# Mirrored blocks of the diagonal score quarters turned by VectorE and DMA in place of TensorE, 36 score blocks multiplied where 38 were, and the row maxima subtracted out of place into a ring of three tiles

## The reference, cut to what matters

```python
lhs = x * w_lhs
rhs = x * w_rhs
scores = jnp.einsum('nsd,ntd->nst', lhs, rhs)
attn = jax.nn.softmax(scores, axis=2)
return jnp.einsum('nst,ntd->nsd', attn, x)
...
h = jax.nn.relu(jnp.einsum('bsh,hi->bsi', hidden_states, W1) + b1)
return jnp.einsum('bsi,ih->bsh', h, W2) + b2
```

## Time and profile before

| what | value |
|---|---|
| median of three executions | 693.37 us |
| profiled execution, span from first to last instruction | 691.5 us |
| instructions | 13488 |
| TensorE matmuls busy | 686.1 us, 99% |
| VectorE busy | 558.4 us, 81% |
| ScalarE busy | 427.5 us, 62% |
| GpSimd busy | 361.7 us, 52% |
| DMA traffic | 77.54 MB, mean 112 GB/s |

### The profile page before, as it was taken

How to read it: one execution, slowest core, us unless ns; L and a number is a source line. 1 busy time by engine, 2 the same in 40 slices (tenths; PEclk the granted TensorE clock), 3 DMA queues, 4 the chain that set the end, 5 groups by cost and what they waited for, 6 DMA issues and landing times.

```text
span 691.5 us, 13488 instructions
## 1 busy us (share of the span) xinstructions
PE 686.1 (99%) x4621; PEld 627.7 (91%) x4621; DVE 558.4 (81%) x1059; ACT 427.5 (62%) x625; POOL 361.7 (52%) x396
## 2 busy tenths in 40 slices
PE   9999999999999999999999999999999999999998
PEld 8688899998999989998999989999899998999997
DVE  5699989799898898978989799887989887876421
ACT  3265398736786367683786647864678634845562
POOL 3572576636654386352872458643665434523644
PEclk9999999999999999999999999999999999999999
DMA  8211761137431382315622266112843126003300
GB/s 294 81 49 59 204 193 55 39 107 252 123 100 56 103 232 91 99 61 179 180 67 90 67 226 185 61 38 98 258 121 99 46 91 221 1 1 100 100 31 30
DMA packets 61663, 77.54 MB, mean 112 GB/s; under 512 B 5632, under 2 KB 54336, under 8 KB 61632
## 3 DMA queue, kind: packets, MB, share of 16 engines
...
HBM read 46.15 MB, written 30.97 MB: 112 GB/s over the span
## 4 chain that ended last, share of the span: by engine, by line
PE 94%; DVE 4%; issue 0%; ACT 0%; DMA 0%; DVEq 0%; ACTq 0%; SPq 0%
PE col L595 9%; PE col L594 9%; PE col L593 9%; PE acc L530 8%; PE acc L531 8%; PE acc L536 8%; PE score L694 8%; PE score L690 8%; PE score L691 8%; PE score L578 4%; PE score L579 4%; PE score L580 4%; PE score L576 2%; PE score L584 2%; PE score L499 1%; DVE S L879 1%
## 5 line engine op out<-in xcount | busy, mean ns | idle before, releaser
L1088 POOL TENSOR_TENSOR hid_lo<-hid,hid_hi 128x512 fp32r<-128x512 f32 x127 | 175.4, 1386 | 143.2 <-ACT hid_hi L719 142.8
L715 ACT ACTIVATE hid<-col,b1T 128x512 f32<-128x512 f32 x128 | 87.0, 679 | 140.3 <-PE col L595 126.1
L530 PE MATMUL acc<-W2hi,hid_hi 128*128 128x256 f32 x480 | 119.2, 282 | 0.0
L531 PE MATMUL acc<-W2lo,hid_hi 128*128 128x256 f32 x480 | 116.9, 278 | 0.0
L690 PE MATMUL score<-V,Phi 128*128 128x258 f32 x448 | 108.8, 281 | 0.0
L691 PE MATMUL score<-V,Phi 128*128 128x256 f32 x448 | 108.6, 281 | 0.0
L719 ACT ACTIVATE hid_hi<-hid 128x512 fp32r<-128x512 f32 x128 | 81.0, 633 | 37.6 <-PE acc L536 29.8
L593 PE MATMUL col<-h2hi,W1hi 128*128 128x512 f32 x256 | 102.4, 400 | 0.0
L595 PE MATMUL col<-h2hi,W1lo 128*128 128x512 f32 x256 | 101.0, 395 | 0.0
L594 PE MATMUL col<-h2lo,W1hi 128*128 128x512 f32 x256 | 100.6, 393 | 0.0
L530 PEld LDWEIGHTS acc<-W2hi,hid_hi 128*128 128x128 f32 x480 | 90.4, 188 | 2.1
...
## 6 DMA issues: line engine op xcount, KB each, us to landing
...
blocks<-block_rows SPq DMA_DIRECT2D x116, 128.0 KB, 3.0
...
lower<-score_blocks SPq DMA_DIRECT2D x56, 128.0 KB, 2.9
...
```

Source lines behind the costliest of these rows:

```text
L530: nc.tensor.matmul(o, hi, W2hi[:, it, :], start=(it == 0 and (apart or t % 2 == 0)), stop=False, skip_group_check=True)
L531: nc.tensor.matmul(o, hi, W2lo[:, it, :], start=False, stop=False, skip_group_check=True)
L715: nc.scalar.activation(hid[:, n % 2, :], col[n % 2][:], ACT.Relu, bias=b1T[:, n % FT:n % FT + 1]).then_inc(col_read, 1)
L1088: G.tensor_tensor(hid_lo[:, n % RING, :], hid[:, n % 2, :], hid_hi[:, n % RING, :].bitcast(F32), ALU.subtract).then_inc(hid_lo_done, 1)
```

## The change

Batch 0 keeps its score steps. In the seven others:

- In a quarter on the diagonal, tiles 0 to 3 now multiply blocks (0, 1, 2), (1, 2, 3), (2, 3) and (0, 3), that is 3, 3, 2 and 2 (the table QCOLS). With the right quarter that is 10 + 16 + 10 = 36 blocks. Tile 3 reads blocks 0 and 3 with a stride.
- The ten turns on TensorE go. The missing six blocks of each such quarter are turned as the lower left quarter is: a new DVE step QT.h turns three pairs of blocks in 32 x 32 pieces into a staging place (6 x 128 columns), SyncE stores it (QW.h) and reads it back in four parts (QR.h).
- S is packed: it holds the multiplied blocks, the turned ones and `lower`.
- The maxima are gathered from parts: DVE's copy writes a row tile's own maximum into `part_max`; MX.0 and MX.2 reduce the six turned blocks of the upper and lower quarter and then all parts; MX.1 reduces `lower` in two pieces.
- The subtraction SB.n writes into `soft`, a ring of three tiles in the place of Plo's ring. It has three instructions: kept blocks, turned blocks, and the other quarter. It now waits for the AV step three tiles back. EX and SM work on `soft`.
- MB.0 now waits for MX.0, and MB.1 for MX.2.
- All tables of order are new.

```diff
-        SC.0 F.0- SC.1 F.1- F.2- SC.2 SC.3 F.3- SC.4 F.4- MB.0 G.0- SC.5 G.1- SC.6 F.5- SC.7 G.2- F.6- G.3-
...
+        SC.0 SC.1 F.0- SC.2 SC.3 F.1- F.2- SC.4 F.3- SC.5 G.0- SC.6 G.1- SC.7 F.4- G.2- F.5- F.6- G.3- G.4-
...
-        SC.0 B2.1- ST.0 SC.1 XG.2- ST.1 VL.0 XG.3- SC.2 L1.0+ SC.3 ST.2 ST.3 SC.4 V.0 T2.1- SC.5 SB.0 SB.1
-        SC.6 SC.7 BH.0+ SB.2 VL.1 SM.0 MX.0 SB.3 V.1 L1.1+ SM.1 SB.4 OUT.0- AV.0 BH.1+ SB.5 AV.1 SM.2 SM.3
...
+        XG.2- SC.0 XG.3- SC.1 B2.1- SC.2 ST.0 ST.1 SC.3 VL.0 QT.0 SC.4 L1.0+ SC.5 ST.2 ST.3 SC.6 V.0 SC.7
+        BH.0+ QT.1 T2.1- VL.1 MX.0 V.1 SB.0 SB.1 SB.2 SM.0 L1.1+ MX.1 SM.1 SB.3 MX.2 AV.0 SM.2 SB.4 OUT.0-
```

```diff
+    QCOLS = [(0, 1, 2), (1, 2, 3), (2, 3), (0, 3)]
+
+
+    UPPER, TURNS = 26, 6
+    PACKED = [0, 3, 6, 8]
+
+    MAX_ORDER = [3, 0, 1, 2]
...
+        turned_q = [s_flat[:, at + h * TURNS * P:at + (h + 1) * TURNS * P].rearrange("p (u s r) -> p s u r", u=Q, r=QP) for h in range(2)]
...
+        lower = s_flat[:, at + 2 * TURNS * P:T * ROWS].rearrange("p (h u v t r) -> p h u v t r", h=2, u=Q, v=HT, t=2)
...
+        with nc.sbuf_tensor("stage", [P, 2, Q, HT, 2, QP], F32) as stage, \
+                nc.sbuf_tensor("stage_lr", [P, T, P], F32) as stage_lr, nc.sbuf_tensor("soft", [P, RING, T, P], F32) as soft:
+            stage_q = [q.rearrange("p a b -> p (a b)")[:, 0:Q * TURNS * QP] for q in (soft[:, RING - 1], stage_lr[:])]
```

SyncE's new steps:

```diff
+                        sp.wait_ge(quarter_done[n], b)
+                        sp.dma_start(quarter_blocks[n], stage_q[n]).then_inc(quarter_stored[n], 16)
...
+                        sp.wait_ge(quarter_stored[n], 16 * b)
+                        for u in range(Q):
+                            cols = slice(u * TURNS * QP, (u + 1) * TURNS * QP)
+                            sp.dma_start(turned_in[n][u * QP:(u + 1) * QP],
+                                         quarter_blocks[n][:, cols].rearrange("(u a) f -> a u f", a=QP)).then_inc(quarter_turned[n], 16)
```

TensorE:

```diff
+                        quarter = QCOLS[n % HT]
+                        lo_tile = n // HT * HT + quarter[0]
+                        for right in range(0 if n < HT else 1, 2):
+                            if right and n == 0:
                                 wait(pe, av_read, T * b)
...
+                            else:
...
-                        for i in range(left // P, at // P):
-                            if i == at // P - 1:
-                                pe.wait_ge(scores_read, T * b + i + 1)
-                            last = nc.tensor.transpose(score[n % 2][:, i * P:(i + 1) * P], S[:, i, n * P:(n + 1) * P], ident[:])
+                                if not right:
+                                    hi, lo = Rhi[:, kk, HR:ROWS], Rlo[:, kk, HR:ROWS]
+                                elif n % HT == HT - 1:
+                                    whole = slice(n // HT * HR, (n // HT + 1) * HR)
+                                    hi, lo = [r[:, kk, whole].rearrange("p (c q) -> p c q", q=P)[:, ::HT - 1, :] for r in (Rhi, Rlo)]
+                                else:
+                                    cols = slice(lo_tile * P, (lo_tile + len(quarter)) * P)
+                                    hi, lo = Rhi[:, kk, cols], Rlo[:, kk, cols]
+                                nc.tensor.matmul(o, Lhi[:, kk, tile], hi, start=(kk == 0), stop=False)
+                                nc.tensor.matmul(o, Lhi[:, kk, tile], lo, start=False, stop=False)
+                                last = nc.tensor.matmul(o, Llo[:, kk, tile], hi, start=False, stop=(kk == DK - 1))
...
+                        else:
+                            pe.wait_ge(max_ready, 2 * b + n - 1)
+                            if n == 0:
+                                pe.wait_ge(scores_read, T * b + HT)
+                            else:
+                                pe.wait_ge(scores_read, T * b + T)
...
+                            o, most = max_ps[:, j * P:(j + 1) * P], n * HT + MAX_ORDER[j % HT]
```

ScalarE:

```diff
+                        else:
+                            tile = soft[:, n % RING, :, :]
...
+                            act.wait_ge(stage_stored[1], 16 * b)
+                        elif n == 2:
+
+                            act.wait_ge(quarter_stored[1], 16 * b)
...
+                        nc.scalar.activation(Phi[:, n % RING, :, :], soft[:, n % RING, :, :], ACT.Copy).then_inc(phi_done, 1)
```

VectorE:

```diff
+                        h, t = n // HT, n % HT
+                        most, width = part_max[:, h, 0, MAX_ORDER[t]:MAX_ORDER[t] + 1], len(QCOLS[t]) * P
...
+                        elif t < HT - 1:
+                            V_.tensor_scalar(s_flat[:, 7 * t * P:7 * t * P + HR + width], score[n % 2][:, 0:HR + width], 1.0, None, ALU.mult, ALU.max,
+                                             accum_out=most).then_inc(scores_read, 1)
+                        else:
+                            V_.tensor_scalar(s_flat[:, 7 * t * P:7 * t * P + HR], score[n % 2][:, 0:HR], 1.0, None, ALU.mult, ALU.max,
+                                             accum_out=most)
+                            V_.tensor_scalar(s_block[:, 20:26:5, :], score[n % 2][:, HR:HR + width].rearrange("p (c q) -> p c q", q=P), 1.0, None, ALU.mult, ALU.max,
+                                             accum_out=part_max[:, h, 3, MAX_ORDER[t]:MAX_ORDER[t] + 1]).then_inc(scores_read, 1)
...
+                        tile, h, t = soft[:, n % RING, :, :], n // HT, n % HT
...
+                        dve.wait_ge(av_done, T * b + max(n - RING + 1, 0))
...
-                        V_.tensor_tensor(tile[:, 0:HT], tile[:, 0:HT], most.broadcast_to([P, HT, P]), ALU.subtract)
-                        dve.wait_ge(scores_turned, 16 * Q * (2 * b + n // 2 - 1))
...
+                        rows = (slice(0, 4, 3), slice(0, 2), slice(0, 3), slice(1, 4))[t]
+                        if h == 0:
...
+                        V_.tensor_tensor(tile[:, h * HT:(h + 1) * HT][:, rows], kept, most.broadcast_to(list(kept.shape)), ALU.subtract)
+
+                        rows, turns = ((slice(1, 3), slice(0, 2)), (slice(2, 4), slice(2, 4)), (slice(3, 4), slice(4, 5)), (slice(0, 1), slice(5, 6)))[t]
+                        out = tile[:, h * HT:(h + 1) * HT][:, rows]
+                        V_.tensor_tensor(by_quarter(out), turned_q[h][:, turns], by_quarter(most.broadcast_to(list(out.shape))), ALU.subtract)
+
+                        if h == 0:
+                            dve.wait_ge(scores_turned[n // 2], 16 * Q * b)
+                            V_.tensor_tensor(by_quarter(tile[:, HT:T]), lower[:, n // 2, :, :, n % 2, :].rearrange("p u v r -> p v u r"),
+                                             by_quarter(most.broadcast_to([P, HT, P])), ALU.subtract).then_inc(sub_done, 1)
+                        else:
+                            V_.tensor_tensor(tile[:, 0:HT], s_upper[:, :, t, :], most.broadcast_to([P, HT, P]), ALU.subtract).then_inc(sub_done, 1)
...
+                        dve.wait_ge(scores_read, T * b + (n + 1) * HT)
+                        if n == 0:
+                            pairs = s_block[:, 5:26, :].rearrange("p (g m) c -> p g m c", m=7)[:, :, 0:2, :]
+                        else:
+                            pairs = s_block[:, UPPER + 1:UPPER + 10, :].rearrange("p (g m) c -> p g m c", m=3)[:, :, 0:2, :]
+                        V_.transpose(stage_q[n].rearrange("p (u g j r) -> p g j u r", u=Q, g=3, j=2),
+                                     pairs.rearrange("p g j (u r) -> p g j u r", r=QP)).then_inc(quarter_done[n], 1)
+                    elif kind == "MX" and n == 1:
+
...
+                        by_row = lower.rearrange("p h u v t r -> p v (h u) (t r)")
+                        V_.tensor_reduce(part_max[:, 1, 3, 0:3], by_row[:, 1:HT], AX.XY, ALU.max)
+                        V_.tensor_reduce(part_max[:, 1, 3, 3:4], by_row[:, 0:1], AX.XY, ALU.max).then_inc(left_done, 1)
                     elif kind == "MX":
...
+                        h = n // 2
+                        dve.wait_ge(quarter_turned[h], 16 * Q * b)
+                        places = part_max[:, h].rearrange("p k a -> p (k a)")[:, HT:HT + 10].rearrange("p (j x) -> p j x", x=HT + 1)[:, :, 0:3]
+                        V_.tensor_reduce(places.rearrange("p j g -> p g j"), turned_q[h].rearrange("p (g j) u r -> p g j u r", j=2), AX.XY, ALU.max).then_inc(parts_done, 1)
+                        wait_apart(dve, scores_read, T * b + (h + 1) * HT)
+                        if h == 1:
+                            wait_apart(dve, left_done, b)
+                        dve.wait_ge(parts_done, 2 * b + h - 1)
+                        V_.tensor_reduce(row_max[:, h * HT:(h + 1) * HT], part_max[:, h].rearrange("p k a -> p a k"), AX.X, ALU.max).then_inc(max_ready, 1)
```

213 lines of the change are left out of this document (110 added, 103 removed).

## The result

The changed kernel takes 739.15 us (median, 736.29 to 739.85) against 693.34: 1.0647 times as long, 95% interval 1.0624 to 1.0669. I had forecast 682.4. The profiled execution has a span of 737.3 us, 45.8 more than before's 691.5. One execution of a kernel further down (e4) took 1363.68 us, nearly twice its three others, and is left out of its median.

What follows compares the result with a forecast made beforehand. TensorE was taken to set the 82.24 us period; 1.86 us less a batch cuts the 691.5 us span by 13.1 to 678.4, plus 2.1 for lateness and 1.9 from span to timed median: 682.4 us, range 679.5 to 685.

Steps and rivals of the forecast that it cites:

- The turns: TensorE, batches 1 to 7: seventy block turns go, 0.115 us each by pitch, 8.1 us in all.
- rival 4: Turns hold TensorE for their recorded 273 ns each: median 669 us; chance within the 0.03 for below 679.
- The two blocks: TensorE, tiles 0 and 4: score products of 384 columns for 512 save 0.7 us a batch, 5.0 in all.
- The counts: Score matmuls in the trace: 384-column ones rise from 84 to 168, 512-column ones fall from 252 to 168.
- DVE's new forms: VectorE's changed steps priced by columns: SC -1.5, SB +0.8, QT +1.7, MX +2.3 us a batch.
- The upper bound of +13.6 us: VectorE's added work a batch if SB, QT and MX pieces cost most; DVE would need 85.1 us.
- the handoffs: Middle batch, waits between engines: airs of 0.4 to 1.4 us, one 0.6 short; the lists fit, but barely.
- 0.3 us of lateness a batch: Allowance for TensorE waiting on late handoffs, bounded by 0 and 1.5 us a batch; 2.1 us in all.
- The 0.6 us that I did find, at SB.2: SyncE's SR.1 lands about 10 us after QT.1; DVE wants it after 9.4, so 0.6 us short.
- DVE's +3.3 us: VectorE's added work a batch: busy 74.8 of 80.4 us, air shrinking from 10.7 to 5.6 us.
- Late handoffs: TensorE waits at MB.0 or AV.0 about 1 us in each of seven batches: 687.3 us; chance 0.19.
- VectorE becomes the bound: DVE's list, middle batches: at +9 us a batch the period is 83.0, time 699; decides from +8.2; chance 0.10.

Runs made afterwards that it cites:

- e4: M with the first half's maximum (MX.0) moved ahead of the second half's ln_v (VL.1) in VectorE's loop table: 708.93 us.
- the part tried: Before without the ten turns in batches 1 to 7, plus 128 columns less in two products of tiles 0 and 4: 683.3 us.
- b1: Before with only SyncE's loop table changed: AM.0 behind XT.0, X1.0 right behind it, ahead of S2.1: 729.48 us, 1.0515.
- M: The changed kernel with only SyncE's middle-batch table reordered by when each transfer is free and wanted, AM.0 first: 707.26 us, 1.0198.
- The two single mends: The changed kernel with, in SyncE's middle table, AM.0 ahead of XT.0 (734.79 us), or SW.1 and SR.1 moved earlier (730.95); both together 712.86.
- e6: M with MX.0 ahead of VL.1, batch 0's old tables, last batch's AV.7 earlier, XG.2 and XG.3 behind evictions, AV.7's read before output adds: 716.01 us.
- e9: M with F.7 ahead of MB.0, F.8 ahead of AV.0, XG.2 and XG.3 each one eviction later, old end tables, last two value products earlier: 696.99 us.
- v1: M leaving out three quarters of the elements in MX.0 and MX.2 from the third batch on: 705.51 us, 1.0162.

## Why the prediction was wrong

**Right.** The turns: 8.1 us forecast, 7.7 measured, at the pitch and not the record's length (rival 4 falls). The two blocks: 0.7 a batch forecast; of the part tried, 0.46, the runs gave 0.38. The counts: 168 score products each of 512, 384 and 256 columns; the strided ones keep the pitch of 0.117 to 0.12 us. DVE's new forms, taken from columns, came within 0.15 us: QT 0.87 forecast plus its overlap, 0.97 and 0.94 recorded; MX 0.94, 1.75, 0.68; pieces of SB 0.28 to 0.68. With every instruction counted up to the start of the next, the changed steps cost DVE 3.0 us a batch in after: SC -1.6, SB +0.8, QT +1.75, MX +2.0, for -1.5, +0.8, +1.7 and +2.3 forecast. The upper bound of +13.6 us was far off.

**The step that failed: the handoffs.** I walked SyncE's queue from QW.1 on, for the upper half's score blocks alone, and allowed 0.3 us of lateness a batch, at most 1.5. Measured: 9.5 in the batch shown, 8.6 to 11.6 in the five. Four things were missing.
- The walk never went through the head of SyncE's table. AM.0 had been first there; it now stood behind XT.0, with X1.0 and S2.1 behind both. The order alone, in one variant, costs before 36 us (b1). In after it costs 32 of 46 (M).
- The 0.6 us that I did find, at SB.2, was 3.25 us. I gave SR.1 3.0 us from its first issue to its last landing (1.7 + 1.3), where the earlier trace rows make it 4.2 (1.3 + 2.9) and after took 7.4. I had judged the DMA by its mean share, "far from full", and took the landings of before.
- I added airs as if lateness were spent once. On queues in fixed order it goes round: SyncE's load holds DVE, DVE's turn holds SyncE's store. The two single mends gave 4.4 and 8.2 us and both together 26.3.
- The sum had no term for the clock. Behind each of five waits of 3.5 to 3.8 us it fell, 1.5 to 2.0 us more each, 8.3 us in all.

**The term that was mis-sized: DVE's +3.3 us.** DVE is busy 76.8 us a batch, 5.3 more than before. The new forms are 3.0 of these, close to what I took; the other 2.3 I had put at nothing. They are in lines whose work the change leaves alone: h2lo +2.2, Plo +0.8, V -0.5, the rest -0.2. By form, in four batches of the loop, before and after (busy us, mean ns):

```profile
L1002 DVE TENSOR_TENSOR h2lo<-featT,h2hi 128x512 fp32r<-128x512 f32 x16 | 10.4, 682 | 0.2 <-ACT h2hi L745 0.2
```
```profile
L1107 DVE TENSOR_TENSOR h2lo<-featT,h2hi 128x512 fp32r<-128x512 f32 x16 | 19.1, 1235 | 0.0
```

h2lo takes 2.2 us more a batch (8.7 in four). Plo's records grow from 39.8 to 43.6 us in four, part of which overlaps the next instruction. GpSimd now works in the same moments: while the two h2lo of 454.09 took 3.78 us, GpSimd ran

```profile
454.34 1.30 POOL L1193 TENSOR_TENSOR hid_lo<-hid,hid_hi 128x512 fp32r<-128x512 f32 x1
455.93 1.39 POOL L1193 TENSOR_TENSOR hid_lo<-hid,hid_hi 128x512 fp32r<-128x512 f32 x1 [0.29 <-ACT hid_hi L772]
```

Two h2lo alone take 1.28 to 1.29; 3.78 is that and the better part of two hid_lo. The Trainium skill (SBUF — State Buffer, Who interferes with whom) says that a VectorE operation with two inputs in SBUF and a GpSimd operation that reads SBUF share a port pair by lock, and the later one waits for the whole of the earlier. The numbers agree with that. The kept traces of all 19 kernels agree too: 419 single h2lo had none of GpSimd's hid_lo, x_cur or ln_t in their time and took 0.66 to 0.70 us, and all 159 that took over 0.8 us had one. For Plo it is 390 at 1.18 to 1.23 us, and all 327 over 1.3 us. So the lengthening goes with GpSimd's work. No run here moved hid_lo away from h2lo, so what that would give back is not shown.

**The rivals.** Late handoffs (0.19) had the place right, MB.0, and put 7 us on it, where the span came out 58.9 us above the 678.4 without waits. "VectorE becomes the bound" (0.10, 699 us) fits M and most forms mended from it, 697 to 709 us (e6 716), with DVE at +4.8 us (e9) to +5.6 (M) and not from +8.2 on, since it needs to be full only between h2lo and SB.0. That reading rests on M's rows and on waits that moved in e4 and v1. My list named the one queue for all transfers in passing and gave no price to a queue that orders two engines' work, and that was the largest part.

**What stays open.** In e9, 3 us above before and 14.6 above the forecast of 682.4, the loop periods stand 1.0 to 2.2 us above 80.4, small stops mostly released by DVE; the rest is in batches 0 and 1 and the last. How much of it is DVE's lengthening beside GpSimd, and whether a table exists in which TensorE's gain shows in the time, wasn't settled.
